# A graph network on one core: the edge loop of its second layer rebuilt as a pipeline over groups of four tiles

## The reference

```
x = layer_norm(relu(norm(nodes)))            # per node, 128 features
s = edge_embeddings + x[center] + x[neigh]   # per edge
h = silu(s) @ phi_w1 + phi_b1
theta_edge = silu(h) @ phi_w2 + phi_b2
agg = segment_sum(x[neigh] * theta_edge, center)
out = silu(x + agg) @ theta_w + theta_b      # per node
```

## Time and profile before

| | us |
|---|---|
| median of 3 timed runs | 13,064.93 |
| lowest and highest | 13,060.98 to 13,084.19 |
| profiled execution, span from first to last instruction | 16,353.9 |

### The profile page before, as it was taken

One profiled execution on the slowest core, in us unless ns is written; L12 is line 12 of the kernel. 1 busy time (PEld: TensorE's weight loads), 2 busy tenths in 40 slices (PEclk: granted clock), 3 DMA queues, 4 the chain that ended last, 5 costly groups with the idle time before them and its releaser, 6 DMA issues. The chain is left out here.

```text
span 16353.9 us, 162092 instructions
## 1 busy us (share of the span) xinstructions
PE 6697.3 (41%) x38666; PEld 5971.1 (37%) x38667; DVE 7103.0 (43%) x23363; ACT 2564.5 (16%) x5999; POOL 6771.6 (41%) x6977
## 2 busy tenths in 40 slices
PE   1013333333333355555555542222223455545544
PEld 0013333333333244444444432222222445544444
DVE  5952222226888544444444442222224344444444
ACT  0001111112222122222222220000001111111111
POOL 0026666661000243443443426666661444444544
PEclk9986666666666677787777766666665555556555
DMA  0224444443333122222212231111122111111214
GB/s 15 91 71 127 129 128 127 126 129 97 80 77 77 53 54 55 54 56 54 56 53 55 56 40 47 46 47 47 47 46 33 47 49 49 51 49 49 52 49 51
DMA packets 1147046, 1069.29 MB, mean 65 GB/s; under 512 B 259528, under 2 KB 972445, under 8 KB 1146656
## 3 DMA queue, kind: packets, MB, share of 16 engines
q0 software_dynamic: 250368, 580.54, 14.1%
q1 hardware_dynamic: 896284, 485.69, 11.0%
q10 hardware_dynamic: 132, 0.83, 0.0%
HBM read 778.93 MB, written 287.53 MB: 65 GB/s over the span
## 5 line engine op out<-in xcount | busy, mean ns | idle before, releaser
L904 POOL DMA_INDIRECT buf<-node_rows,buf x3504 | 3431.1, 979 | 2939.5 <-PE psum L1837 1332.4
L904 POOL DMA_INDIRECT buf<-node_rows_ln,buf x1728 | 1666.1, 964 | 4163.7 <-ACT buf L1269 1934.0
L599 POOL DMA_INDIRECT edge_rows_by_src<-buf x1728 | 1671.9, 968 | 1065.4 <-ACT buf L609 547.4
L918 PE MATMUL psum<-buf 128*128 128x129 f32 x3456 | 647.5, 373 | 1946.1 <-DMA buf<-node_rows,buf 1929.7
L646 PE MATMUL psum<-buf 128*128 x3456 | 722.0, 375 | 1670.7 <-ACT buf L618 1017.6
L918 PEld LDWEIGHTS psum<-buf 128*128 128x128 f32 x3456 | 628.4, 285 | 1965.3 <-issue 1009.0
L1837 PE MATMUL psum<-buf 128*128 128x132 f32 x3456 | 633.8, 366 | 1692.1 <-DVE buf L1907 1595.1
L646 PEld LDWEIGHTS psum<-buf 128*128 128x128 f32 x3456 | 651.2, 280 | 1725.9 <-issue 1725.7
L897 DVE TENSOR_SCALAR buf<-buf 128x128 f32<-128x128 f32 x5216 | 1117.3, 293 | 318.4 <-issue 287.7
L1837 PEld LDWEIGHTS psum<-buf 128*128 128x128 f32 x3456 | 615.9, 276 | 1740.9 <-issue 1740.9
L928 DVE TENSOR_TENSOR buf<-buf,psum 128x129 f32 x864 | 250.7, 290 | 1619.8 <-DMA buf<-in_edge_attr 1472.6
(11 more groups left out here) (287 smaller groups left out, 13217.8 us busy)
## 6 DMA issues: line engine op xcount, KB each, us to landing
buf<-edge_rows_by_src SPq DMA_DIRECT2D x114, 1056.0 KB, 8.4
buf<-edge_rows_by_src SPq DMA_DIRECT2D x110, 1024.0 KB
buf<-in_edge_attr SPq DMA_DIRECT2D x864, 128.0 KB
buf<-loc_rows_by_dst SPq DMA_DIRECT2D x112, 512.0 KB
buf<-node_rows,buf POOLq DMA_INDIRECT x3504
edge_rows_by_src<-buf SPq DMA_DIRECT2D x139, 260.0 KB, 2.6
edge_rows_by_src<-buf POOLq DMA_INDIRECT x1728
buf<-node_rows_ln,buf POOLq DMA_INDIRECT x1728
```

The source lines that it names most:

```text
L599: nc.gpsimd.indirect_dma_start(rows, bass.IndirectOffsetOnAxis(ap=at[:, h, t:t + 1], axis=0), st[:, h, t, :], None).then_inc(scattered[h], 16)
L904: nc.gpsimd.indirect_dma_start(rows[:, t, 0:used], None, table, bass.IndirectOffsetOnAxis(ap=stage[:, t:t + 1], axis=0)).then_inc(sem, 16)
L918: last = nc.tensor.matmul(ps[:, q // 3, (q % 3) * W:(q % 3) * W + width], oh[:, 2 * q + s, :], rows[:, 2 * q + s, 0:width], start=(s == 0) ...
```

## The change

In `l1_edges` the unit is now the group of four tiles. Every engine runs a step per group, and in a step each stage works on a different group: one-hots five groups ahead, `ea + xn` four ahead, silu and the transposed sum three ahead, w1 two ahead, w2 and the message one ahead, pair sums and their running total at zero. `xn` and `ea` have eight buffers of one group each; POOL gathers group j when the message of the group eight before is ready. The loop body has eight groups (two halves).

- The edge sum is built transposed in PSUM: four transposes of `ea` (into which `xn` has been added in place), then for each pair three bf16 products of a third of the node table (`tab3`: high, middle and low part of the fp32 value) with the one-hot turned by 256 edges. ACT's silu reads this PSUM directly. The PE transposes of one-hots, ACT's copies of them, DVE's second addition, and ACT's copy of the transposed sum are gone.
- The turned one-hot comes from a row of positions for each half (bf16, 128 x 2048), which SP loads by broadcast from `loc_rows_by_src`; DVE compares it with the partition's number.
- The pair sums are not added to a block of `agg`: DVE runs them on in a ring of 16 pairs, `new = old * keep + pair sum`, keep being 0 where a block begins, and SP stores eight pairs (512 KB) per half to `running_sums` in DRAM.
- `l1_nodes` makes `tab3`, `keep` and `loc_by_src`; `l1_finish` loads the node table back and, with one transfer for each of the 49 blocks, the running sum of the block's last pair; `rank_phase` writes those pair numbers.

```diff
-        for g in range(4):           # one half, before
-            turn_onehot(nc, c, oh[:, h], psH, g).then_inc(ohT_ps, 1)
...
+    if inside(i, j, 3):                                  # TensorE
+        pe.wait_ge(partial, BODY * i + (j + 4))
+        for t in range(TG):
+            nc.tensor.matmul(psS[:, g % 2, t * P:(t + 1) * P], ea[:, g, t, :], c["ident"][:], is_transpose=True, start=(t == 0), stop=False)
+        for q in range(PG):
+            for k in range(3):
+                last = nc.tensor.matmul(psS[:, g % 2, 2 * q * P:(2 * q + 2) * P], tab3[:, bass.ds(blocks[q], 1), k, :]..., turned[:, h, first:first + 2 * P], ...)
+    if inside(i, j, 2):
+        pe.wait_ge(sT_ready, BODY * i + (j + 3))
+        nc.tensor.matmul(psH[:, 0], w1[:], sT[:, j % 2], start=True, stop=True)
+    if inside(i, j, 1):          # theta of group j + 1: four products with w2
+    if inside(i, j, 0):
+        pe.wait_ge(msg_ready, BODY * i + (j + 1))
+        pe.wait_ge(added, BODY * i + (j - 1 + ADDED))
+        ...                      # four products for two pair sums
...
+    pool.wait_ge(msg_ready, BODY * i + (j + 1 - BODY))   # GpSimd, a group
+    for t in range(TG):
+        nc.gpsimd.indirect_dma_start(xn[:, j, t, :], None, table1, ...).then_inc(got[j], 16)
...
+    # VectorE, step j, in this order
+    tensor_scalar(oh[:, g5, ...], iota, loc_st, is_equal)          x4
+    if j % 4 == 3: tensor_scalar(turned[:, h, :], locs[:, h, :], number, is_equal)
+    tensor_tensor(ea[:, g4], ea[:, g4], xn[:, g4], add)
+    tensor_tensor(m, psT, b2, add); tensor_tensor(msg, msg, xn, mult)
+    scalar_tensor_tensor(ring[:, p], ring[:, p - 1], keep_st, psA, mult, add)   x2
...
+    with sp.Fori(0, NI) as i:                                      # SyncE
+        for h in range(2):
+            sp.wait_ge(turned_hot, ...);  locs_of(2 * i + (h + 2), h)
+            sp.wait_ge(s_ps, ...);        edges_of(2 * i + (h + 2), h)
+            sp.wait_ge(added, ...);       sp.dma_start(running[...], ring[...])
```

More of the change, by code:

```diff
@@ L391, in _ @@
                 pool.sem_inc(consts, 1)
[L392 removed]
+                pool.wait_ge(in_dram, 32)
                 pool.wait_ge(run_known, 1)
@@ L1157, in norm_nodes, with l1_nodes @@
     ch.link(nc.vector.tensor_tensor(dst, dst, bc(st["nmr"][:].unsqueeze(2), sh), ALU.add))
-def l1_nodes(nc, c, ins, table1):
+def l1_nodes(nc, c, ins, blk_rows, table1, tab3, keep, loc_by_src):
     es = ExitStack()
@@ L1219, in l1_edges, with inside, over_bodies @@
+        def inside(i, j, ahead):
+            return not isinstance(i, int) or 0 <= BODY * i + j + ahead < NG
+        def over_bodies(eng, step, first):
+            for j in range(BODY + first, BODY):
+                step(-1, j)
+            with eng.Fori(0, NI - 1) as i:
+                for j in range(BODY):
+                    step(i, j)
+            for j in range(BODY):
+                step(NI - 1, j)
         with nc.Block() as block:
@@ L1244, in _ @@
+                nc.gpsimd.iota(number[:], [[1, 1]], base=0, channel_multiplier=1, allow_small_or_imprecise_dtypes=True).then_inc(numbered, 1)
+                for j in range(BODY):
+                    gather(0, j, False)
+                with pool.Fori(1, NI) as i:
+                    for j in range(BODY):
+                        gather(i, j, True)
             @block.scalar
             def _(act):
-                act.wait_ge(loaded, 64)
-                for h in range(2):
-                    nc.scalar.copy(stage[:, h], c["idx"][:, h * HALF:(h + 1) * HALF]).then_inc(staged, 1)
@@ new lines, in _ @@
+                dve.sem_inc(biased, BIASED)
+                dve.sem_inc(added, ADDED)
+                dve.sem_inc(halfway, HALFWAY)
+                dve.sem_inc(keep_staged, KEEP)
+                for h in range(2):
+                    nc.vector.tensor_copy(stage[:, h], c["idx"][:, h * HALF:(h + 1) * HALF]).then_inc(staged, 1)
+                nc.vector.tensor_copy(loc_st[:, 0], c["loc"][:, 0:HALF]).then_inc(loc_staged, 4)
+                nc.vector.memset(ring[:, PB - 1, :], 0.0).then_inc(cleared, 1)
@@ L1389, in l1_finish @@
+                dve.wait_ge(loaded, 64)
+                dve.wait_ge(numbered, 1)
+                dve.wait_ge(blank, 16)
+                over_bodies(dve, step, -5)
+def l1_finish(nc, c, ins, table1, running, last_pairs):
     es = ExitStack()
@@ L1401, in _ @@
                 sp.dma_start(b[:], row_of(ins["L1_gnn_theta_b"]).broadcast_to([P, D])).then_inc(loaded, 16)
-                sp.wait_ge(loaded, 32)
+                sp.dma_start(tab[:, :, 0:D], table1.rearrange("(b p) d -> p b d", p=P)).then_inc(loaded, 16)
+                sp.dma_start(last_pair[:], last_pairs).then_inc(known, 16)
+                sp.wait_ge(known, 16)
+                for first in range(0, NB, KB):
+                    pairs = nc.values_load_multi_w_load_instructions(
+                        last_pair[0:1, first:first + KB], engines=[ENG.SP], min_val=0, max_val=NPAIR,
+                        skip_runtime_bounds_check_because="a block's last pair is below NPAIR, that of an empty block is NPAIR")[1]
+                    for k in range(KB):
+                        sp.dma_start(agg[:, first + k:first + k + 1, 0:D], running[:, bass.ds(pairs[k], 1), :]).then_inc(loaded, 16)
+                sp.wait_ge(loaded, 48 + 16 * NB)
             @block.scalar
```

373 lines of the change are left out of this document (217 added, 156 removed).

## The result

| | us |
|---|---|
| before, median of 4 runs | 13,065.42 (13,060.98 to 13,084.19) |
| after, median of 4 runs | 12,618.12 (12,583.29 to 12,625.56) |
| ratio | 0.965, 95% interval 0.9638 to 0.9662 |
| after, profiled execution | 12,583.29, span 12,581.5 |

The account below looks back on a forecast made before the run. The prediction took layer 1's edges to be bound by the order of their work, no engine being full. Its terms: 13,065 - 3,050 + 2,393 + 49 = 12,457, forecast 12,460 us, range 11,950 to 12,980.

Parts of the forecast that it names:

- The likeliest case: Layer 1's edges: POOL sets the pace after the change, 5.47 us a group; total 12,460 us, chance 0.78.
- Layer 1's edges in the timed runs of before: That stage before the change, without the profiler: between 2,992 and 3,327 us, taken as 3,050.
- The serial half: Layer 1's edges before: 19.1 and 8.6 us of handed-over work, 27.7 us a half, floor 2,992 us.
- the 335 us that were left over: Timed 9,868 us for the four gather or scatter stretches, beyond floors of 9,533; a fifth was given to layer 1.
- The stage after: Layer 1's edges after the change: 432 groups at 5.47 us plus 30 for filling and draining, 2,393 us.
- Outside the loop: Added cost: `tab3` in `l1_nodes` 14, `l1_finish` 33, pair numbers and `keep` 2; together 49 us, bounds 30 to 90.
- What PE, DVE and ACT were said to need: Layer 1's edges after, per group: PE 4.9 us, DVE 4.0 (4.3 with waits), ACT 1.38, all below POOL's 5.47.
- The gather has 31 us of 44.: New layer 1 pipeline: gather, landing and steps to its message need 31 us of the 44 that eight groups give.
- Everything shrinks alike: Whole kernel: all stages shrink equally outside the profiler, so the stage saves 1,382 us; total 11,680, chance 0.07.
- DVE starves POOL: Layer 1's edges after: gathers stop during DVE's SBUF work, 7.5 us a group; total 13,335, slower, chance 0.06.
- PE the bound: Layer 1's edges after: half clock, 9 us a group, 14,000 total; or bf16 products at 0.51, 13,030; chance 0.04.
- The stalls are real in timed runs: Layer 1's edges after: compute slows beside gathers, 10.8 us a group, stage 4,650; total about 13,590, chance 0.05.

Follow-up runs that it names:

- the kernel with two queues: Changed kernel with `l1_finish`'s 49 transfers divided between SyncE's and ScalarE's queues, pair numbers loaded first: 15,228.88 us, ratio 0.913 to the kernel before.
- the run with thin loads: Changed kernel loading in the loop one of 16 tiles of edge features per half: 12,607.55 us, ratio 0.9647 to the kernel before.
- the second profile of before: The kernel before, unchanged, profiled once more: 13,074.99 us, span 13,073.2.
- the kernels built on the changed one: Changed kernel with ScalarE's turned one-hot (ratio 0.9163), `l1_finish` transfers on two queues (0.913), or both (0.9138; on a further chip 0.9231), against the kernel before.

## Why the prediction was right, and where it was off

The likeliest case came true: POOL sets the pace, and the time is 12,618 us where 12,460 stood. The difference, step by step:

- **Layer 1's edges in the timed runs of before.** 3,050 us was taken, 2,857 is right: 193 us too much, the largest error. Two parts. The serial half was not a floor: 27.7 us was read around a stall in one half, 27.2 is a half without one and 26.4 the mean, (27.7 - 26.45) x 108 = 135 us. And of the 335 us that were left over, none belonged to layer 1 (58 taken). Above their floors were layer 3 by 321 us, layer 2 by 82 and `spread_phase` by 72, and layer 1 was 136 below its own. Layer 3 is also paced by POOL, but the floor took a gather at 0.945 us, and there the mean is 1,088 ns, which is 254 of the 321. The prediction had a 1.85 us gather of this very layer before it. It charged that price to the new stage and not to the floor of layer 3, and so left too much for layer 1.
- **The stage after.** 2,393 us forecast, 2,309 measured, 84 less. POOL's 4 x 1.25 = 5.0 a group held. Longer gathers were put at 0.37 us a group; (995 - 944) x 4 = 0.20 came. The release of each group was put at 0.1; POOL's idle time of 563.9 / 432 = 1.31 a group against 4 x 0.30 gives 0.1. Sum 5.29, 2,284 us, and 25 for filling and draining, where 30 stood.
- **Outside the loop.** 49 us forecast. From the start of layer 0's edges to that of layer 1's it is 4,944.7 - 3,256.2 = 1,688.5 us against 4,930.3 - 3,257.2 = 1,673.1: 15 more, of which `l1_nodes` has 12 and layer 0 the rest. From the end of layer 1's edges to the start of layer 2's it is 7,455.4 - 7,253.4 = 202.0 against 7,936.8 - 7,786.5 = 150.3, so `l1_finish` grew by 52: the transfers cost 0.69 us each and not 0.6, and 17 us pass before the first, for which the term held nothing. Together 67.
- **The sum.** With the measured terms the forecast's own sum is 13,065 - 2,857 + 2,309 + 67 = 12,584. The profiled execution took 12,583. The median is 35 us higher, and what the traces show of that is layer 3's edges, which took 2,536 us in one execution and 2,573 in another with the same code. The errors partly hid one another: 193 us too much was taken for before and 84 too much for after. That the forecast lay only 158 us below the median is in part luck.
- **What PE, DVE and ACT were said to need.** PE 4.9 us a group with 4.6 as the least, measured 3.74 in the timeline and 3.83 where it binds. The six bf16 products were put at 1.2, measured 0.82; the rest is that the rows of PE were added up though they overlap. The Trainium skill (TensorE: Matmul & The Clock Gate, "Back-to-back issue gap") was closer: in the timeline of the kernel with two queues four such products in a row span 0.60 us and six 0.82, so 0.11 each, which is what its rule gives. DVE 4.0 to 4.3, measured 1,576 / 432 = 3.65. Of this the turned compare is 0.13, as on bf16 it took 0.75 us and not 1.28; its rows too overlap a little, and that is most of the rest. ACT 1.38, measured 1.29. None of these counts, as PE with four products fewer showed; PE was the bound only with half of the gathers left out.
- **SP, landings and bytes.** Said to be hidden; the run with thin loads shows it for the edge features, the largest of SP's transfers. The DMA share was put at 0.45 and came to 0.57.
- **"The gather has 31 us of 44."** Right in that eight in flight are enough and six as well. But the count was loose: what decides is the number of DVE steps between the releasing message and the adding of the rows, five, three or one.

The rivals. *Everything shrinks alike* (11,680) fell with the measured time and with the second profile of before: the stretch without gathers kept its length (1,673 us, and 1,672 in the earlier trace rows), and only those with gathers shrank. *DVE starves POOL* (13,335) fell in size: gathers average 995 ns with DVE busy for 68% of the stage. The mechanism is there, but small: cutting the compare took 17 ns off the mean gather. The Trainium skill (SBUF — State Buffer, "SBUF: two separate sides") has POOL fully blocked during DVE's instructions of the kinds that it lists; by that rule a group would have lost far more than the measured 0.20 us (the fp32 one-hots alone take 383.8 / 432 = 0.89), unless most of the gather's 0.94 us needs no port. No run here separates these. *PE the bound* fell: the clock was 0.91, and a third of its bf16 products were enough for the same stage.

*The stalls are real in timed runs* is the one that must be told in full. The prediction said that the 3,289 us "exist only under the profiler". Such stalls exist without it: on two chips the kernel before took 16,674 and 16,284 us timed, and on a chip where it takes 13,066 a profile shows 13,073. The first profile of before (16,354) looks like one from the former; on which chip it was taken is not on record. Each chip was seen in one session, so the runs don't tell whether the stalls belong to the chip or to its condition at the time. For the forecast the mistake was without effect, since in the runs that it was made for the kernel before took 13,065. The rival's price was wrong: on such a chip the stage was to grow to 4,650 us and the kernel to be slower. It came to 2,889, and the kernels built on the changed one were faster by 7.7% to 8.7%, more than elsewhere. The 2.5-fold stretch of all computing was this rival's failed step. It is PE's signals that are late, by some us, while the instructions of DVE, ACT and POOL keep their length. A chain of hand-overs pays for each late one: 4,172 - 2,856 = 1,316 us in the first profile of before. The pipeline with several groups in flight pays 2,889 - 2,309 = 580. The changed kernel itself was not run on such a chip, only versions that differ from it by 20 us or so.

Why PE's signals are late there, and only in stages in which POOL gathers or scatters, no run shows.

## What to carry to other kernels

When the hand-overs of a stage are on its path, more buffers and a schedule in which each engine works on another group gain up to the pace of the slowest engine; test for this by halving one engine's work before and after the change, and two runs name the bound. When a profile is longer than the timed runs, take another profile before anything is subtracted from it: the mean of a stage from an undisturbed one would have removed most of this forecast's error. And count the depth of a pipeline in steps between release and need: four in flight cost 2,000 us here, six cost nothing.

## What the hardware showed that was not expected

- The same program took 13,065 and 13,066 us on two chips and 16,284 and 16,674 on two others, steadily within each session. All of the difference lies in stages with gathers or scatters. In the edges of layer 1 it is PE's signals that come late (5.02 and 4.61 us in the rows above, 0.04 in the profile of after), while those of DVE and ACT come on time.
- Gathers lengthen beside DVE's work by a little, not by its duration: a mean of 995 ns with DVE busy for 68% of the stage, 978 with the turned compare cut from 750 ns to 281, 957 where POOL waits for over half of the stage. In layer 3's edges the mean was 1,088.
- A DVE compare from bf16 to bf16, 128x2048, took 750 ns; from bf16 to f32 it had taken 1.28 us.
